# The last expert of a mixture-of-experts layer: where the next linear layer's weight blocks are turned

## What is computed

```python
# second layer: 8 experts, each takes its (at most 314) rows; two experts per row
h = relu(einsum('ecd,edh->ech', disp, w1) + b1[:, None, :])     # 1024 -> 512
out = einsum('ech,ehd->ecd', h, w2) + b2[:, None, :]            # 512 -> 1024
y = einsum('tk,tkd->td', gates_k * valid, out[idx_k, loc_c])
x = x + y
# third layer: a linear layer with W (1024 x 1024), then a sum over the graph's edges
h = einsum('nd,od->no', layernorm(x), W) + b
```

## Time and profile before

| | us |
|---|---|
| median of 3 runs | 1155.72 |
| lowest and highest | 1146.02 and 1159.23 |
| the profiled execution | 1151.9 |
| its span, first to last instruction | 1150.2 |
| PE busy in it | 1018.0 (89%) |
| DVE busy | 748.1 (65%) |
| ACT busy | 443.2 (39%) |

### The profile page before, as it was taken

The page is one execution under the profiler, slowest core; times in us unless marked ns, Lnnn a source line. Parts: engine busy times, 40 slices in busy tenths (PEclk is TensorE's granted clock), DMA queues, the critical chain, the costliest instruction groups (busy, mean ns, idle before and its releaser), DMA issues.

```text
span 1150.2 us, 17894 instructions
## 1 busy us (share of the span) xinstructions
PE 1018.0 (89%) x6895; PEld 559.8 (49%) x6895; DVE 748.1 (65%) x1035; ACT 443.2 (39%) x540; POOL 158.4 (14%) x216
## 2 busy tenths in 40 slices
PE   0799699993899999997299989989899999999997
PEld 0688554441666666565144434444444444444443
DVE  7999668888455555564687637777746555555540
ACT  3388535452344444455112126646504222111111
POOL 6200053331300000000433000010100000000000
PEclk9899889997699999999699989989999999999999
DMA  4567316634856777663579527766510454444440
GB/s 142 191 221 256 112 74 214 228 133 176 264 194 236 269 251 256 242 230 116 162 172 200 131 92 233 248 208 228 179 37 10 101 129 110 109 109 109 110 92 33
DMA packets 170193, 189.97 MB, mean 165 GB/s; under 512 B 130665, under 2 KB 130987, under 8 KB 166031
## 3 DMA queue, kind: packets, MB, share of 16 engines
q1 hardware_dynamic: 163727, 166.52, 46.9%
q0 software_dynamic: 6400, 22.55, 6.6%
HBM read 137.98 MB, written 35.86 MB: 151 GB/s over the span
## 4 chain that ended last, share of the span: by engine, by line
PE 65%; DVE 19%; DMA 6%; issue 5%; ACT 2%; POOL 2%; SPq 1%; DVEq 0%; ACTq 0%; POOLq 0%
PE ps L1210 12%; PE ps L1181 11%; PE ps L1167 9%; PE ps L1096 8%; PE ps L1004 8%; PE ps L1114 5%; DVE stats L1614 3%; DVE xn L1767 2%; PE ps L1070 2%; DMA eo_d<-eo 2%; DVE fq L2126 2%; DVE w1l L1947 1%; PE ps L1153 1%; PE ps L901 1%; DVE xl L1777 1%
## 5 line engine op out<-in xcount | busy, mean ns | idle before, releaser
L1210 PE MATMUL ps<-w2q,hqt 128*128 128x512 fp8e4 x640 | 140.8, 379 | 1.6 <-DVE out_t L2182 1.4
L1181 PE MATMUL ps<-w1q,xqt 128*128 128x512 fp8e4 x640 | 139.9, 379 | 1.4 <-issue 1.4
L1495 ACT ACTIVATE hf<-ps,fs 128x512 f32<-128x512 f32 x80 | 54.9, 687 | 183.6 <-PE ps L1181 183.6
L2163 DVE TENSOR_REDUCE hm<-hf 128x1 f32<-128x512 f32 x80 | 54.2, 685 | 76.3 <-ACT hf L1495 76.3
L1181 PEld LDWEIGHTS ps<-w1q,xqt 128*128 128x128 f16 x640 | 62.5, 98 | 76.7 <-issue 1.9
L1210 PEld LDWEIGHTS ps<-w2q,hqt 128*128 128x128 f16 x640 | 62.3, 98 | 76.1 <-DVE out_t L2182 1.9
L1004 PE MATMUL ps<-wt_h,xt 128*128 128x512 f16 x320 | 86.3, 383 | 0.0
L1004 PE MATMUL ps<-gwt_h,xt 128*128 128x512 f16 x320 | 83.4, 382 | 0.8 <-DMA xt<-xt_d 0.8
L2126 DVE SCALAR_TENSOR_TENSOR fq<-fnat_a,sw,fsgn 128x1024 fp8e4<-128x1024 f32 x48 | 60.6, 1282 | 33.2 <-ACT fsgn L1464 16.7
L1096 PE MATMUL ps<-xdh,w1h 128*128 128x314 f16 x256 | 77.5, 303 | 3.5 <-DVE w1l L1947 2.7
L1096 PE MATMUL ps<-xdl,w1h 128*128 128x314 f16 x256 | 76.7, 299 | 0.0
(11 more groups left out here) (291 smaller groups left out, 2005.6 us busy)
## 6 DMA issues: line engine op xcount, KB each, us to landing
abs_in<-in_L_ffn_w SPq DMA_DIRECT2D x32, 1024.0 KB, 6.1
wstage<-in_L_ffn_w SPq DMA_DIRECT2D x32, 1024.0 KB, 10.1
fnat_a<-in_L_ffn_w SPq DMA_DIRECT2D x48, 512.0 KB, 4.8
eo_d<-eo SPq DMA_DIRECT2D x16, 512.0 KB, 2.9
bias_b<-in_L_ffn_w SPq DMA_DIRECT2D x16, 512.0 KB, 4.2
hq_d<-hq SPq DMA_DIRECT2D x8, 1024.0 KB, 6.3
xs_d<-xs_all SPq DMA_DIRECT2D x10, 512.0 KB, 3.0
out_x<-out_t SPq DMA_DIRECT2D x9, 512.0 KB, 2.6
```

Of the source, the lines that this page charges most:

```text
L1181: last = mm(ps[:, n % 4, :], xqt[:, u, k, :], w1q[:, k // 2, n * 512:(n + 1) * 512, k % 2], start=(k == 0), stop=(k == KD - 1))
L1210: last = mm(ps[:, 4 + h, :], hqt[:, u, k, :], w2q[:, k // 2, h * 512:(h + 1) * 512, k % 2], start=(k == 0), stop=(k == KF - 1))
L1495: cp(hf[:, i % 2, n * 512:(n + 1) * 512], ps[:, n % 4, :], ACT.Gelu, scale=fs[:, i % 2, 3:4]).then_inc(s_ge, 1)
L2163: last = v.tensor_reduce(hm[:, u, n:n + 1], hf[:, u, n * 512:(n + 1) * 512], AX.X, ALU.max, apply_absolute_value=True)
```

## The change

PE turns blocks 0 to 3 behind the first to fourth second product and blocks 4 to 7 behind the last product; between the first products it turns none. ACT and DVE take their steps in a matching order: behind the first activation only block 1 is split, and everything else follows behind the fourth. On DVE, each of the first four result rows now stands ahead of a copy and a low part (of the block two further on) instead of behind. SP sends the loads of blocks 2 and 3 ahead of the stores, those of blocks 4 and 5 behind the first row tile's store and those of blocks 6 and 7 behind the second's, ahead of the last four stores.

```diff
@@ SP, expert(e, ep)
                 if last_of(e, NE):
-                    for i in range(2, KD - 1):
-                        w1_rows(i)
+                    w1_rows(2)
+                    w1_rows(3)
@@
                         sp.dma_start(expert_rows[e][s * P:s * P + SM[s], :], eo[0:SM[s], u, :]).then_inc(s_eout[u], 16)
-                        if s == 0 and last_of(e, NE):
-                            w1_rows(KD - 1)
+                        if last_of(e, NE):
+                            w1_rows(4 + 2 * s)
+                            w1_rows(5 + 2 * s)
@@ PE, expert(e, ep)
                     last.then_inc(s_g1, 1)
-                    if last_of(e, NE) and hb >= 1:
-                        w1_t(hb - 1)
@@
                         if last_of(e, NE):
-                            w1_t(3 + 2 * s + h)
+                            w1_t(2 * s + h)
@@
                 last.then_inc(s_g2, 2)
                 if last_of(e, NE):
-                    w1_t(KD - 1)
+                    for i in range(4, KD):
+                        w1_t(i)
@@ ACT, expert(e, ep)
                     cp(hth[:, hb, :], ht32[:, hb % 2, :], ACT.Copy).then_inc(s_hh, 1)
-                    if last_of(e, NE):
-                        w1_high(hb + 1) if hb < 2 else w1_part(hb - 2)
+                    if last_of(e, NE) and hb == 0:
+                        w1_high(1)
                 if last_of(e, NE):
-                    for i in range(3, KD):
+                    w1_part(0)
+                    for i in range(2, KD):
                         w1_high(i)
                         w1_part(i - 1)
                     w1_part(KD - 1)
@@ DVE, last_expert(e, ep)
                     v.tensor_tensor(htl[:, hb, :], ht32[:, hb % 2, :], hth[:, hb, :], ALU.subtract).then_inc(s_hl, 1)
-                    w1_low(hb + 1) if hb < 2 else w1_part(hb - 2)
+                    if hb == 0:
+                        w1_low(1)
                 dve.wait_ge(s_b2, 16 * e + 16)
                 for n in range(4):
-                    w1_low(3 + n)
-                    w1_part(2 + n)
                     result_rows(e, ep, n // 2, n % 2)
-                w1_low(KD - 1)
+                    w1_part(n)
+                    w1_low(2 + n)
                 result_rows(e, ep, 2, 0)
                 result_rows(e, ep, 2, 1)
-                w1_part(KD - 2)
-                w1_part(KD - 1)
+                for i in range(4, KD):
+                    w1_part(i)
+                    if i + 2 < KD:
+                        w1_low(i + 2)
```

## The result

The changed kernel takes 1145.03 us (median of 22 runs, 1139.64 to 1155.11); the kernel before, run beside it as often, 1151.45 us (1144.42 to 1161.16). The ratio is 0.9938, with a 95% interval of 0.991 to 0.9965: some 7 us less, with 4 to 10 us inside the interval. The profiled execution took 1146.21 us, against 1151.9 us of the one before.

What follows compares the result with a forecast made beforehand. PE, holding 65% of the chain, was taken to bound the kernel up to the last product. 10.84 - 0.5 - 0.4 - 0 = 10 us off a median of 1155.7 gave 1145.7 us, range 1139 to 1151.5.

Steps and rivals of the forecast that it cites:

- The first products: PE, last expert: without three blocks, their two stalls and half clock, four products take 12.84 us, 10.84 us less.
- the fourth quarter: First second product on PE: last hidden rows there at 522.1, needed at 522.3, so no stall, some 0.2 us spare.
- The second products: PE and DVE: no block waits; last product ends at 537.15, last result rows start at 537.7, shift 10.3 us.
- Rivals one and three: One: tail or transfers eat part, 1150 us, chance 0.17. Three: result rows behind load 5's low part, slower, 0.03.
- The last stores: SP's queue: loads 6 and 7 under way beside the last four stores cost 0.4 us, bounds 0 and 0.9.
- those land within 2.5 us: Sign on SP: load 7 leaves ahead of the last stores, and these stores land within 2.5 us.
- the shift at the gathers: POOL's gathers behind the last stores: 10.0 us earlier, from 10.3 us less the stores' delay.
- The tail: Blocks 4 to 7 behind the last product: copied by 546.8, cost 0, bounds 0 and 1.5 us.
- a limit of 548.4: Tail's latest free end: the second mix, on the chain, starts at 549.7, less 1.28 us.
- The clock in the tail: PE's tail transposes run at the low level: 1.2 us more of tail, ending at 548.0, nothing of the time.
- The linear layer: Moves whole with the chain; rival two, it takes the gain back: 0 to 4 us remain, 1152 to 1156, chance 0.07.
- the fourth: Rival: stalls often longer, linear layer's first product meets high clock earlier; up to 3 us more, 1142 to 1143, chance 0.08.

Runs made afterwards that it cites:

- The early loads: Changed kernel with loads 4 to 7 sent once the fourth first product is done, into places of their own: 1143.54 us, ratio 0.9932.

## Why the prediction was right, and where it was not

**The first products.** Right. 12.84 us were worked out for the four; from 507.23 to the first second product at 520.07 it was 12.84. No stall at the fourth quarter.

**The second products.** Right to the tenth: the last product's end at 29.6 us after the start (worked out 29.6), the last result rows' start at 30.18 (30.2). The reason was given correctly too: DVE's order, and ahead of it ACT, which has the copy of block 3 in front of load 5's split. The early loads, which left these rows where they were, show that load 5's landing does not matter here. Rivals one and three count from that landing; by the prediction's own sum it had 1.4 us to spare (534.0, against 535.4 for the end of ACT's copy) before they could begin.

**The last stores.** Here the sum failed. The term was 0.4 us with bounds of 0 and 0.9, from stores of 512 KB that took 3.5 us beside loads and 2.6 us without. It was 1.7 us in the profile (3.27 less 1.59), and so the sign "those land within 2.5 us" failed; over five profiles of kernels with the changed order of loads the last store took 2.9 to 3.9 us, against 1.5 to 1.6 in those with no load in flight. The large store was too kind a row for small ones: loads in flight added 0.9 us to its 2.6, but 1.3 to 2.3 us to the 1.6 of the small ones behind them. With 1.7 in its place the shift at the gathers would have been 8.6 us. The first gather started 45.4 to 45.9 us after the start in four profiles with the old order, and 36.7 to 37.4 in five with the changed one: 8.7 us between the means.

**The tail.** It cost nothing, but by luck in the size. It was worked out to end at 546.8 with a limit of 548.4; it ended at 549.2, and the second mix still had 0.42 us to wait (0.15 in the second profile of this kernel). Counted from the start the tail ended at 41.9 us, 1.0 us behind the forecast's limit of 40.9; it was hidden only because the late stores had moved the gathers, and the limit with them, to 42.3. Load 6 was sent at 535.85, as assumed, but ACT could split it only at 541.22 and stood idle for 2.2 us before: 5.4 us of landing and not 3.6, with the second tile's store ahead of it and load 7 behind.

**The clock in the tail.** PE's timeline of the changed kernel, blocks 5, 6 and 7:

```profile
539.14 0.61 PE L1080 MATMUL ps<-id,gnh 128*128 128x128 f16 x8 [1.26 <-ACT gwt_h L1402]
...
543.34 1.01 PE L1080 MATMUL ps<-id,gnh 128*128 128x128 f16 x8 [3.05 <-ACT gwt_h L1402]
...
546.56 1.01 PE L1080 MATMUL ps<-id,gnh 128*128 128x128 f16 x8 [1.26 <-ACT gwt_h L1402]
```

Blocks 4 and 5 ran at the high level (2.4 GHz), 6 and 7 at the low one (1.2 GHz), after an idle time of 3.05 us. It cost the tail at most 0.8 us a block, and the kernel's time nothing. The Trainium skill (TensorE: Matmul & The Clock Gate, What's actually happening) has the clock follow how busy PE has been lately. The trace agrees in that the tail ends at the low level; that the whole tail runs there, as the prediction drew from it, holds for two blocks of four.

**The linear layer.** It was said to move whole, with a chance of 0.07 that it takes the gain back. Both are too simple. Without transfers that turn rows it does move whole (117.4 and 117.0 us). With them each execution draws a landing time between 7 and 13 us, and a long one costs 2.2 to 6 us of the layer (two of them 9.3). Before, the third product's input came just in time, 0.27 us late: a tie of two paths. The prediction did not look at this wait. Both paths gained from the change, for the transfer's issue moved with the rest; but with no room between them each late landing goes straight into the time. In the kernel's time the step cost little in the middle, presumably because the kernel before has such landings too; that is argued from its two profiles, not shown.

**The number.** 1145.7 was forecast, 1145.03 measured. That is closer than the steps deserve: the cut was 10 us in the forecast and 7 (4 to 10) in the measurement, and the median of before was 1155.72 in the runs shown and 1151.45 in 22. Within 1% was given 0.59, and it is within 1%. Of the rivals, the first came true in part, and by another way: the transfers took 1.3 us more than the 0.4 allowed, at the stores and not at load 5. The third and the fourth found nothing for them: the last result rows never waited for a load, and the layer's first product did meet the high clock earlier (a pair of matmuls took 0.59 us from 5.3 us after the layer's first transposes, at 566.07; in the earlier trace rows it was 7.5 us), but then its result rows had to wait for a busy DVE.

**What stays open.** Whether a late transfer is more likely when the layer starts earlier. Landing times over 11 us were seen in one of four profiles with the old order of loads and a transfer in the layer (the two of the kernel before, and those with load 2 early and with the third tile by PE), and in three of seven with the blocks moved; PE waited over 2 us for one in two of the four and in five of the seven. That is too few to say. What makes a transfer late was not found either; gathers and stores run beside every one of them. One mark goes with it: in each of these seven profiles with a wait over 2 us one of SP's issues of a store to xt_d, behind the transfer, took 1.9 to 5.1 us, in the other four none took over 0.7. It may be a result of the lateness and not its cause.

## What to carry to other kernels

- Work that waits for two other engines' copies does not belong between the products of an engine that bounds the kernel, where its copies queue behind results that are still being computed. Placed where the queue is empty it costs its own time alone (0.89 us a block here), and behind the last product nothing, as long as its end lies before the next stage's first need; here half a microsecond was left, and when the last copy came 3.3 us later, the second mix came 3.0 us later.
- A load that is issued just ahead of the stores that end a stage lengthens them. Look for room to send it earlier rather than later.
- Where a chain passes a wait of almost nothing, two paths are tied there. Even where a change moves both, the scatter of the tied path becomes the kernel's.

## What the runs showed of the hardware

- Four small stores (two of 96 KB, two of 20 KB) land 1.5 to 1.6 us after the issue of the last with no load in flight (eight profiles), and 2.9 to 3.9 us after it with two loads of 512 KB ahead (five profiles).
- Transfers of 512 KB that turn rows took 4.3 to 13.3 us from issue to landing, the same one (the fourth tile's, kernel before) 8.86 in one execution and 13.33 in another. Behind PE's waits for them, of 2.6 to 6.7 us, the granted clock fell to the low level for a while: 0.84 in the ten microseconds from 590 in the changed kernel, where a product took 12.3 us in place of 10.4.
